# A four-layer kernel on one core: a copy moved ahead of two products in local attention, a diagonal mask written by four quarter matmuls, and an input copy moved ahead of indirect transfers

## What is computed

```python
# layer 0, mixer: latent attention, 8 heads, causal, keys and values from a latent of 32
k_lat = (x @ wk_down).reshape(Bq, Tq, N_KV, D_LAT)
scores = jnp.where(causal, scores, jnp.finfo(scores.dtype).min)
probs = jax.nn.softmax(scores, axis=-1)
# layer 3, branch: twice over: local attention with windows of 64, 8 heads of 64, then a gated FFN
q = l2norm(q) * qs
k = l2norm(k) * ksc
q, k = rotary_xpos(q, k)        # q * cos * scale + rotate_half(q) * sin * scale
o = local_attention(q, k, v)    # window of 64 and the one before it
x = x + o @ wo
```

## Time and profile before

| what | value |
|---|---|
| median of three runs | 3042.26 us |
| profiled execution | 3024.94 us |
| its span, first to last instruction | 3023.0 us |
| TensorE matmul busy | 2741.2 us, 91% |
| VectorE busy | 2122.7 us, 70% |
| ScalarE busy | 1950.8 us, 65% |
| GpSimd busy | 1046.4 us, 35% |
| mean granted TensorE clock | 0.959 |

### The profile page before, as it was taken

How to read it: one execution, slowest core, us unless ns; L and a number is a source line. 1 busy time by engine, 2 the same in 40 slices (tenths; PEclk the granted TensorE clock), 3 DMA queues, 4 the chain that set the end, 5 groups by cost and what they waited for, 6 DMA issues and landing times. The chain is left out here.

```text
span 3023.0 us, 67408 instructions
## 1 busy us (share of the span) xinstructions
PE 2741.2 (91%) x21388; PEld 1809.0 (60%) x21388; DVE 2122.7 (70%) x3740; ACT 1950.8 (65%) x5578; POOL 1046.4 (35%) x1228
## 2 busy tenths in 40 slices
PE   6799999997989789888789999998988999999898
PEld 3577897773654434435556666676435666666644
DVE  4566565666764679757678888886447888888767
ACT  4466565666753654353388888887437888888744
POOL 0233343330000544210055555554215555555431
PEclk9799998998999989889999999999999999999999
DMA  4200120000000000130000000000000000000000
GB/s 141 75 20 21 50 71 25 18 21 8 9 16 0 1 0 1 28 60 1 26 1 0 0 0 0 0 0 13 7 8 2 0 0 0 0 0 0 1 21 35
DMA packets 82996, 51.58 MB, mean 17 GB/s; under 512 B 28848, under 2 KB 75568, under 8 KB 82864
## 3 DMA queue, kind: packets, MB, share of 16 engines
q1 hardware_dynamic: 78768, 41.56, 4.9%
q0 software_dynamic: 4096, 8.40, 0.9%
HBM read 31.59 MB, written 18.35 MB: 17 GB/s over the span
## 5 line engine op out<-in xcount | busy, mean ns | idle before, releaser
L2147 ACT ACTIVATE probs<-banks,minus_max,rnorm 128x128 f32<-128x128 f32 x1024 | 460.1, 469 | 3.4 <-DVE minus_max L2243 3.4
L2018 PE MATMUL banks<-weights,hf 128*128 128x512 f32 x768 | 432.6, 647 | 24.8 <-POOL hf L462 13.5
L2061 POOL TENSOR_TENSOR qk_cross<-qk_raw,rope_scaled 128x512 f32<-128x512 f32 x256 | 325.5, 1272 | 34.5 <-DVE minus_max L2243 14.4
L2223 DVE COPY probs_t<-banks 128x512 f32<-128x512 f32 x256 | 176.2, 688 | 128.2 <-PE banks L1996 127.6
L2071 POOL TENSOR_TENSOR qk_rot<-qk_rot,rnorm 128x512 f32<-128x512 f32 x128 | 133.4, 1042 | 325.9 <-DVE qk_rot L2276 318.1
L2147 ACT ACTIVATION_READ_ACCUMULATOR probs<-banks,minus_max,rnorm 128x1 f32 x1024 | 222.7, 217 | 0.0
L834 ACT ACTIVATE probs<-banks,minus_max 128x128 f32<-128x128 f32 (+1 forms) x512 | 207.9, 425 | 14.3 <-DVE minus_max L873 12.2
L1996 PEld LDWEIGHTS banks<-ident,probs 128*128 128x128 f32 x1024 | 126.9, 141 | 135.2 <-issue 101.4
L2010 PE MATMUL banks<-v_tok,probs_t 128*64 128x64 f32 x3072 | 173.4, 228 | 22.7 <-DVE probs_t L2223 22.7
L2257 DVE TENSOR_REDUCE sumsq<-qk_sq 128x16 f32<-128x1024 f32 x128 | 154.8, 1209 | 26.9 <-issue 19.9
L2267 DVE TENSOR_TENSOR qk_rot<-qk_raw,rope_scaled 128x512 f32<-128x512 f32 x256 | 166.9, 693 | 5.7
(11 more groups left out here) (353 smaller groups left out, 7094.8 us busy)
## 6 DMA issues: line engine op xcount, KB each, us to landing
sorted_x<-zero_rows SPq DMA_DIRECT2D x10, 512.0 KB, 6.2
rows_in<-sorted_x SPq DMA_DIRECT2D x18, 256.0 KB, 3.0
sorted_y<-rows_out SPq DMA_DIRECT2D x18, 256.0 KB, 2.4
x_res<-in_x SPq DMA_DIRECT2D x8, 512.0 KB, 6.5
out_x<-x_res SPq DMA_DIRECT2D x16, 256.0 KB, 2.0
w1b<-in_L_ffn_w SPq DMA_DIRECT2D x8, 256.0 KB, 4.4
s_branch<-in_L_ffn_w SPq DMA_DIRECT2D x8, 256.0 KB, 6.4
w1g<-in_L_ffn_W SPq DMA_DIRECT2D x8, 256.0 KB, 3.0
```

Of the source, the lines that this page charges most:

```text
L2018: pe.matmul(ps[:, misc(k, j)], hf[:, n // 2 % 2, 0, n % 2 * P:(n % 2 + 1) * P], wqkv[:, w:w + QW], start=True, stop=True).then_inc(*S[name ...
L2061: return pool.tensor_tensor(by_half(tw[:, n, at]), by_half(qk[:, n, at])[:, :, ::-1, :], tab[:, n, 2 * w + 1].rearrange("p (a d) -> p a d" ...
L2147: last = act.activation(pr[:, k % 2, head], ps[:, 2 * (k % 2) + par, c * P:(c + 1) * P], ACT.Exp, scale=rn[:, k % 4, head:head + 1], bias= ...
L2223: dve.tensor_copy(pt[:, h], ps[:, 4]).then_inc(*S["turned_sb"].inc)
```

## The change

Three edits.

- In `local_attention`, VectorE copies the second half of the turned probabilities ahead of the two straight products of the rotation; before, it did so behind them.
- In `pe_scores` of `latent_attention`, the whole-array mask product of 384 columns for each head is gone. The products of queries and keys now come first (the wider one with `start=True`), and the mask is added last, to the two diagonal blocks alone. It takes four matmuls of 64 rows by 64 columns of the array, with 256 moving columns each, one for every quarter of the array. The tile `hide` holds two pieces in place of three and is made by four small VectorE instructions in place of two.
- On GpSimd in `latent_attention`, the copy into `xf` comes ahead of the unit's transfers, and the last of the four transfers waits until the queries of the next unit are copied (`q_sb`).

```diff
-             "wvd": buf("wvd", P, N_KV * LAT), "hide": buf("hide", P, 3, P, dt=BF16), ...
+             "wvd": buf("wvd", P, N_KV * LAT), "hide": buf("hide", P, 2, P, dt=BF16), ...
...
-                for qb in range(2):
-                    dve.tensor_copy(w["hide"][:, qb:1 + 2 * qb],
-                                    m["causal"][:, qb, 0:(qb + 1) * P].rearrange("p (k t) -> p k t", t=P))
+                low, high, causal = slice(0, 64), slice(64, P), m["causal"]
+                dve.tensor_scalar(w["hide"][low, 0], causal[low, 0, 0:P], -1e30, None, ALU.max)
+                dve.tensor_scalar(w["hide"][low, 1], causal[low, 1, 64:64 + P], -1e30, None, ALU.max)
+                dve.tensor_scalar(w["hide"][high, 0], causal[high, 0, 64:64 + P], -1e30, None, ALU.max)
+                dve.tensor_scalar(w["hide"][high, 1], causal[high, 0, 0:P], -1e30, None, ALU.max)
...
             for e in range(2):
-                pe.matmul(ps[:, b0 + e, 0:W], one[:], hide[:].rearrange("p k t -> p (k t)"), start=True, stop=False)
+                rows = slice(32 * (2 * s + e), 32 * (2 * s + e) + 32)
+                pe.matmul(ps[:, b0 + e, P:W], qt[rows, u, c, P:T], kt[rows, u, c, :], start=True, stop=False)
             for e in range(2):
                 rows = slice(32 * (2 * s + e), 32 * (2 * s + e) + 32)
-                pe.matmul(ps[:, b0 + e, P:W], qt[rows, u, c, P:T], kt[rows, u, c, :], start=False, stop=False)
+                pe.matmul(ps[:, b0 + e, 0:P], qt[rows, u, c, 0:P], kt[rows, u, c, 0:P], start=False, stop=False)
             for e in range(2):
-                rows = slice(32 * (2 * s + e), 32 * (2 * s + e) + 32)
-                mm = pe.matmul(ps[:, b0 + e, 0:P], qt[rows, u, c, 0:P], kt[rows, u, c, 0:P], start=False, stop=True)
+                rows = slice(64 * e, 64 * e + 64)
+                for h in range(2):
+                    mm = pe.matmul(bank(ps, b0 + e, 3, P)[64 * h:64 * h + 64, ::2], one[rows, rows],
+                                   hide[rows, h:h + 1].to_broadcast([64, 2, P]), start=False, stop=True)
...
-                        if here(i, u, 2):
-                            for t in itertools.islice(tiles, TOK // (2 * pairs)):
-                                move(pool, t)
                         if here(i, u + 2, 2):
                             at = (i * 2 + 2 * first_pair + u + 2) * T
                             pool.wait_ge(*S["v_ps"].at(i, u))
                             pool.tensor_copy(xf[:, u], m["xn"][:, at:at + T]).then_inc(*S["copied"].inc)
+                        if here(i, u, 2):
+                            for t in itertools.islice(tiles, TOK // (2 * pairs) - 1):
+                                move(pool, t)
+                            if here(i, u + 1, 2):
+                                pool.wait_ge(*S["q_sb"].at(i, u + 1))
+                            move(pool, next(tiles))
...
                         dve.tensor_scalar(ss[:], ss[:], 1e-24, None, ALU.max).then_inc(*S["v1"].inc)
+                    if here(i, k - 1):
+                        turned(i, k - 1, 1)
                     if here(i, k + 2):
...
                         last.then_inc(*S["straight"].inc)
-                    if here(i, k - 1):
-                        turned(i, k - 1, 1)
```

More of the change, by code:

```diff
@@ L504, in first_layer @@
         w = {"wq": buf("wq_lat", P, 2, P), "wk": buf("wk_lat", P, 2, 4, LAT), "wv": buf("wo_lat", P, 2, P),
-             "wvd": buf("wvd", P, N_KV * LAT), "hide": buf("hide", P, 3, P, dt=BF16), "one": buf("ident_bf", P, P, dt=BF16)}
+             "wvd": buf("wvd", P, N_KV * LAT), "hide": buf("hide", P, 2, P, dt=BF16), "one": buf("ident_bf", P, P, dt=BF16)}
         r = {"lg": buf("logits", P, TOK, EXPERTS), "prob": buf("prob", P, TOK), "pos": buf("row_of_token", P, TOK, dt=U32),
```

## The result

| | kernel before | changed kernel |
|---|---|---|
| median of four runs | 3041.80 us | 2963.38 us (2963.22 to 2964.76) |
| profiled execution | 3024.94 us | 2963.22 us |
| span | 3023.0 us | 2961.2 us |

The ratio is 0.9746, 95% interval 0.9729 to 0.9763: the changed kernel is 78 us faster where 61 us were forecast, and 2963 us lies 1.4 us inside the lower end of the range (2962 to 3008). A gain of 78 us is above the 48 to 76 us of the likeliest case; gains over 76 us had been given a chance of 0.03. The profiled executions differ by 61.7 us, which is the sum that was forecast. So there are two questions: whether 61.7 us is made up as forecast, and where the other 17 us come from.

A forecast was written before the change was run, and what follows sets the result against it. TensorE was taken to bound latent attention; in local attention three engines were close, so waits mattered. Terms of -51 us (local), -10 us (mask) and zero (input copy) took the median from 3042.26 to 2981 us, range 2962 to 3008.

The forecast's parts named there:

- the likeliest case: Whole kernel: the summed gain arrives, between 48 and 76 us (2966 to 2994 us); chance 0.68.
- The sum: Whole kernel: -51 us local attention and -10 us latent attention give -61 us; 2964 us profiled, 2981 us median.
- Second copy ahead: Local attention: the early copy removes TensorE's wait, 122 slots x (0.47 - 0.05) = -51 us; bounds -66 and -25.
- the wait itself: Local attention: TensorE's wait for the turned probabilities' second half, mean 0.30 us listed, 0.47 us with 0.17 added.
- The ties: Local attention: rotation's sum, residual sum and ScalarE's list come near to binding next; 0 to 0.15 us a slot, 0.05 taken.
- The residual sum: Local attention: its 0.67 us margin before the key transposes shrinks to 0.05 us, less than the hand-over.
- Mask by quarters: Latent attention: mask in four quarters, added last, saves 0.08 us a step, -10 us over 128 steps; bounds -26 and +27.
- Input copy: Latent attention, GpSimd: the copy into `xf` ahead of the transfers brings nothing; zero.
- Half of the gain: Rival: the ties close early, local attention gains only 25 us and latent 10; 3007 us, chance 0.18.
- The second half was what TensorE waited for: Rival denied this: something else holds the mixing, local attention's slots stay at 9.02 us; 3032 us, chance 0.03.
- The quarters don't run in sequence: Rival said they do, or expose their loads: latent attention +27 us, 3018 us with local attention's gain; chance 0.05.
- The copy did not wait for TensorE: Rival said VectorE's early second copy waits for TensorE, delaying work behind it: slower than before, 3067 us; chance 0.03.

The follow-up runs named there:

- hf_late: Changed kernel with GpSimd's copy of `hf` made to wait until the rotation's sum is done; 2974.4 us, ratio 0.9787 to the kernel before.
- full_last: Changed kernel with the mask still last, but by two whole-array matmuls of 256 columns instead of four quarters; 2953.5 us, ratio 0.9716 to the kernel before.
- full_warm: Changed kernel with two whole-array mask matmuls, plus unread matmuls in TensorE's idle time ahead of and starting latent passes; 2933.7 us, ratio 0.9714 to the kernel before.
- after: The changed kernel with all three edits, in the first comparison with the kernel before; 2963.38 us, ratio 0.9746.
- after_again: The changed kernel, unchanged, timed again beside the kernel before; 2961.7 us, ratio 0.9733.
- copy_mid: Changed kernel with VectorE's second copy between the two straight products instead of ahead of both; 2959.1 us, ratio 0.9733 to the kernel before.
- mask_only: Kernel before with the mask edit alone (four quarters, added last); 3019.8 us, ratio 0.9992.
- mask_again: Kernel before with the mask edit alone, run once more in another comparison; 3016.9 us, ratio 0.9988.
- pool_only: Kernel before with the GpSimd edit alone (input copy ahead of transfers, last transfer behind the queries); 3019.9 us, ratio 0.9996.
- quarters_twice: Changed kernel with the four quarter matmuls of the mask issued twice in each step; 2974.1 us, ratio 0.9839 to the kernel before.

## Why the prediction was right, and where not

**The sum.** -61 us was forecast, -61.7 us is the difference of the profiled executions. Of the spans' -61.8 us, -56.9 us lie in the stage of local attention (1508.61 and 1451.76 us from its first matmul to its last), -4.6 us in the passes, and -0.4 us elsewhere. So the sum came out by luck: local attention gave 6 us more than forecast and latent attention 6 us less. The step that made the forecast 2981 and not 2963 us is its last: "on the median, which lies 17 us above it". The 17 us were carried over to the changed kernel, whose median and profiled execution agree. In two of four comparisons the kernel before doesn't show them either. That the range held, by 1.4 us, is luck too: none of its terms stands for the 17 us.

**Second copy ahead.** The mechanism held in each point: the wait for `probs_t` is gone, VectorE reaches the copy without idle time, ScalarE's idle time ahead of `qt` falls from 0.48 us to nothing or up to 0.29 us. The size was -51 us and is -57 us, or -61 where the clock between the layers does not stay low for longer. The term that was too small is the wait itself. Four slots have lost 0.49 us each after the ties, and the ties cost 0.22 us in one slot of four, 0.055 us on the mean, so 0.54 to 0.55 us was there to be removed in place of 0.47. This is the upper bound of the prediction ("if all four slots of a round wait like the one shown"). The list's mean of 0.30 us plus 0.17 was too low, and the difference of two group starts, 1.08 - 0.52 = 0.56 us, was right.

**The ties.** 0.05 us a slot, and 0.055 measured, but not for the reason given. The rotation's sum is late for TensorE in one slot of four only, one of the two in which GpSimd copies `hf`, because the two straight products then take 1.48 us in place of 1.28. In the slots without that copy the sum is in time. From the copy of the first half to the sum are 1689.66 - 1685.71 = 3.95 us, and were 1721.13 - 1717.21 = 3.92, so it is 0.03 us later and not 0.12 to 0.20. The dependence itself costs what the prediction said at the least: the products end at 1689.63 and the sum starts at 1689.66, 0.03 us behind, where an instruction that waits for nothing starts 0.08 us before the end of the one ahead. But the copy and the products start earlier: 1687.74 - 1685.71 = 2.03 us behind the copy of the first half, where they stood 1719.32 - 1717.21 = 2.11 us behind it. The rule of the Trainium skill that was weighed (page "VectorE: DVE Perf Modes", section "The DRAIN you can't avoid") says that the semaphore between them costs nothing extra. These rows don't bear it out: from copy to sum are 1689.66 - 1687.74 = 1.92 us in the new order and were 1721.13 - 1719.32 = 1.81 us in the old, for the same three instructions. The residual sum costs nothing in the changed kernel (PE's waits for it are 1.5 us in 4 times) but is close: `hf_late` made it the bound.

**Mask by quarters.** The estimate of -0.08 us a step came out at -0.085, and two of its terms were measured: 0.105 us for four quarters side by side (forecast 0.12), and 0.13 us for what else they cost (forecast 0.10 for the extra change of form). The Trainium skill says that a change of tiling mode drains TensorE, without a price (page "TensorEngine Tiling (Array Packing)", section "Key Properties"); the 0.13 us fit it. But -10 us became -4.6, and 1 to 4 us in the medians of the mask alone. The step that failed is "over 128 steps": it takes every step to be at the full clock and nothing else in a pass to change. A pass's first two to four steps don't run at the full clock with the mask first, and three to six don't with the mask last. Against 0.085 us for each of 128 steps, 6.3 us are missing in the changed kernel: 3.9 us at the starts of the passes and 2.7 us at their ends (the 2 times 48 steps between gave 0.2 us more). By the granted clock, with the mask last the level rises 25.3 to 30.2 us behind the pass's first matmul in 12 of 16 passes and 16.5 to 16.8 us in the other four, in seven kernels with quarters and in `full_last`. With the mask first it rises 11.3 to 20.2 us behind, in ten passes of five kernels. The part of TensorE's idle time in this is shown by `full_warm`; why the order of the mask delays the rise is not. The 1.5 us at the end of a pass (the stall of VectorE and ScalarE) occur in both passes of `after`, `after_again`, `copy_mid`, `hf_late` and `full_last`. They don't occur in `mask_only`, `mask_again` or `pool_only`, so neither edit of this stage has them by itself, and not in `quarters_twice` or `full_warm` either, which have both edits. Their cause is open.

**Input copy.** Zero, and `pool_only` measured 0.9996 (0.9986 to 1.0005). That holds for the edit by itself; with the mask's edit beside it, the stall at the end of a pass appears in five of seven profiled executions.

**The rivals.** Half of the gain did not come: local attention gained more than forecast. The second half was what TensorE waited for. The quarters don't run in sequence: four take 0.105 us and not 0.43. The copy did not wait for TensorE in any slot that was read, and `copy_mid` shows over 0.6 us of room on its other side.

## What to carry to other kernels

A wait in the middle of an engine's list is best priced by the starts of the groups around it, against the same groups where nothing waits, and over a whole round of slots; the listed mean was a seventh too low. Where three engines are close, read a move twice: for what is next on the same engine, and for what the others now run at the same time. Moving one instruction out of an overlap (`hf_late`) moved those behind it into another, and cost more. A shorter step is worth its count only where the clock is up: before trimming a stage's steps, look at the granted clock of its first 20 us, where filling TensorE's idle time brought 14.5 us over two passes. And before a median and a profile are used in one sum, see that the profiled execution lies among the timed ones.

## What was not expected of the hardware

- GpSimd's copy of 64x255 takes 397 ns in the kernel before and in `hf_late`, and 768 ns (in `copy_mid` 910 ns at the median) beside VectorE's products and sums of two SBUF operands, which go from 1.28 to 1.48 us for two products and from 1.23 to 1.30 us for the sum. In `hf_late` a VectorE maximum of 128x8 that starts 0.07 us behind a GpSimd product of 128x512 takes 1.22 us in place of 0.31, and ends 0.02 us behind it.
- TensorE's clock was at 1.2 GHz for up to 26 us behind a pass's first matmul in the changed kernel, and 30 us in `quarters_twice`, although TensorE was busy for all of 106 to 116 us. With matmuls in the 11.6 us of idle time ahead of the first pass and in its first two waits, it was at 2.4 GHz for all but that pass's first projections.
- Four quarter matmuls of 256 columns take 0.105 us behind four others of their form, and 0.24 us between products on 32 rows and whole-array transposes. Two whole-array matmuls of 256 columns in their place were cheaper by 0.053 and 0.044 us a step.
- The kernel before takes 3020.6, 3021.1, 3039.2 or 3041.8 us in four comparisons, while the kernel with the moved copy alone (two of them) or with all three edits (the other two) takes 2962 to 2964 us.
